# A four-layer graph network on one core: boundaries of layers 1 and 2, rows at the end, and a bias moved from TensorE to VectorE

## The reference

```
layer 0  Wh = h@W; p = softmax(leaky(s_i + d_j), masked); attn@Wh, and a dense branch with gates
layer 1  agg = (adj @ h) / deg;            out = agg @ W.T + b
layer 2  h = h@W; p = softmax(leaky(e_src_i + e_dst_j), masked); out = elu(p @ h)
layer 3  S = (X@Wq)@(X@Wk).T, masked with adj + I; out = softmax(S) @ (X@Wv)
```

## Time and profile before

| what | value |
|---|---|
| three runs, median (lowest to highest) | 2343.1 us (2340.27 to 2345.26) |
| the profiled execution, its own time | 2346.69 us |
| its span | 2345.0 us |
| PE busy | 2225.0 us (95%) |
| DVE busy | 1798.9 us (77%) |
| ACT busy | 1372.6 us (59%) |
| opening and layer 0 | 0 to 921.9 us |
| layer 1 (its block) | 921.9 to 1207.5 us |
| layer 2, to its last `ag` row | 1207.5 to about 1641 us |
| layer 3, rest | to 2345.0 us |

### The profile page before, as it was taken

One profiled execution on the slowest core, in us unless ns is written; L12 is line 12 of the kernel. 1 busy time (PEld: TensorE's weight loads), 2 busy tenths in 40 slices (PEclk: granted clock), 3 DMA queues, 4 the chain that ended last, 5 costly groups with the idle time before them and its releaser, 6 DMA issues. The chain is left out here.

```text
span 2345.0 us, 45615 instructions
## 1 busy us (share of the span) xinstructions
PE 2225.0 (95%) x17180; PEld 1701.0 (73%) x17180; DVE 1798.9 (77%) x2845; ACT 1372.6 (59%) x2100; POOL 114.6 (5%) x124
## 2 busy tenths in 40 slices
PE   5799999999999998999978999999999999999998
PEld 4677767778677776888867888887466666666667
DVE  6877788797877855212249999997898898898896
ACT  6555565665656565666655555554365565665556
POOL 2000010010100001000000000000000000000000
PEclk9899999999999999999989999999999999999999
DMA  7542340414321112222211222222111011111000
GB/s 178 113 64 37 64 82 32 82 46 82 56 62 47 39 57 84 83 89 89 89 38 58 68 67 72 79 73 85 54 37 50 26 52 52 35 46 50 25 30 28
DMA packets 62934, 146.72 MB, mean 63 GB/s; under 512 B 10023, under 2 KB 14778, under 8 KB 61757
## 3 DMA queue, kind: packets, MB, share of 16 engines
q1 hardware_dynamic: 56461, 110.57, 15.2%
q0 software_dynamic: 5760, 33.56, 8.7%
q10 hardware_dynamic: 560, 0.52, 0.1%
HBM read 170.30 MB, written 41.43 MB: 90 GB/s over the span
## 5 line engine op out<-in xcount | busy, mean ns | idle before, releaser
L193 PE MATMUL bank<-s_row,kT_hi 128*128 128x512 f16 x1024 | 308.0, 383 | 5.3 <-ACT arena L2038 3.1
L2152 PE MATMUL bank<-VB,arena 128*128 128x257 f16 x1024 | 281.8, 275 | 26.1 <-DVE arena L2078 20.1
L1560 PE MATMUL bank<-VA,ph 128*128 128x257 f16 x1024 | 281.2, 275 | 8.7 <-DVE VA L1169 8.7
L2859 PE MATMUL bank<-VA,w_dense 128*128 128x257 f16 x1024 | 280.7, 274 | 3.0 <-ACT w_dense L2683 2.4
L1562 PE MATMUL bank<-VA,pl 128*128 128x257 f16 x1024 | 280.8, 274 | 0.0
L1561 PE MATMUL bank<-VA,ph 128*128 128x257 f16 x1024 | 280.8, 274 | 0.0
L2155 PE MATMUL bank<-VB,arena 128*128 128x257 f16 x1024 | 280.7, 274 | 0.0
L2153 PE MATMUL bank<-VB,arena 128*128 128x257 f16 x1024 | 280.6, 274 | 0.0
L2861 PE MATMUL bank<-VA,arena 128*128 128x257 f16 x1024 | 280.2, 274 | 0.0
L2860 PE MATMUL bank<-VA,w_dense 128*128 128x257 f16 x1024 | 280.2, 274 | 0.0
L2017 ACT CAST arena<-arena 128x512 f16<-128x512 f32 x256 | 155.8, 617 | 153.4 <-DVE arena L2069 144.1
(11 more groups left out here) (344 smaller groups left out, 4935.9 us busy)
## 6 DMA issues: line engine op xcount, KB each, us to landing
mask<-mask_d SPq DMA_DIRECT2D x128, 256.0 KB, 2.7
arena<-mask_d SPq DMA_DIRECT2D x128, 256.0 KB, 2.7
mask_d<-in_adj POOLq DMA_DIRECT2D x8, 2048.0 KB, 23.4
xg<-in_x SPq DMA_DIRECT2D x8, 512.0 KB, 12.8
x<-xg SPq DMA_DIRECT2D x8, 512.0 KB, 3.9
xg<-x SPq DMA_DIRECT2D x8, 512.0 KB, 4.3
x<-xo POOLq DMA_DIRECT2D x8, 512.0 KB, 3.0
w_dense<-x SPq DMA_DIRECT2D x8, 512.0 KB, 4.3
```

The costliest lines, as they stand in the source:

```text
L193: last = nc.tensor.matmul(out_ap, st, mv, start=(i == 0), stop=(i == len(todo) - 1))
L1560: nc.tensor.matmul(acc, ph[:, u % HR, c], v_row(V, 0, t), start=(t == 0), stop=False)
L2152: nc.tensor.matmul(acc, p_hi, v_at(V, 0, t), start=first, stop=False)
L2859: nc.tensor.matmul(acc, ph[:, u % ring, j, c], v_row(V, 0, t), start=(t == 0), stop=False)
```

## The change

Five edits. (1) The p tiles of layer 0 and the mask rings of layers 1, 2 and 3 become one tile, `quad_ring`; so the last quad of masks of layer 1's first group is loaded in layer 0's block, as soon as the p tiles are free, and layer 1 doesn't load it again; PE takes this quad tile by tile and not by banks. (2) Wq and Wk are loaded behind layer 1's loop and not before it. (3) In layer 2, `late` is 1: the reciprocals, the `ag` rows and the ELU's Relu come one quad later in the order of DVE and ACT; `arena` is smaller by the masks. (4) The last two pairs of layer 3 are summed bank by bank, and each bank is inverted, scaled and added in one go by DVE and stored by SP (128 KB). (5) Layer 1's bias is loaded once, spread over the partitions, and added to `xg` by DVE; the ones product goes.

```diff
+        quad_ring = sb(top, "quad_ring", [P, R * GW], F32)
...
+        quad_masks = quad_ring[:, :].bitcast(U8).rearrange("p (a n) -> p a n", n=R * GW)
...
-                p32 = sb(mem, "p32", [P, PR, GW], F32)
+                p32 = quad_ring[:, :].rearrange("p (t n) -> p t n", t=PR)
...
                                 load_later()
+                                sp.wait_ge(low.sem, low.upto(G * T - 1))
+                                slot = NEXT % R
+                                sp.dma_start(quad_masks[:, slot, :], mask_d[0:P, NEXT * QW:(NEXT + 1) * QW]
+                                             ).then_inc(s_mask[slot], 16)
...
-                mask = quad_masks(arena[0]) if weighted else sb(mem, "mask", [P, MS, R * GW], U8)
+                mask = quad_masks
                 ring = 4 if weighted else 2
-                late = 0 if weighted else 0
+                late = 1 if weighted else 0
...
                         eng, stage = (dve_q, "p32") if weighted else (act_q, "hi")
+                        if not weighted and isinstance(g, int):
+                            return
...
-                    groups(sp, quad, work["sync"], None, work.get("sync_between"))
+                    if "sync_before" in work:
+                        work["sync_before"](sp)
+                    groups(sp, quad, work["sync"], None, None, work.get("sync_beside"))
...
-                        if q == 0:
+                        if q == late:
                             work["sums_free"](act, g)
                             for r in range(R):
                                 act.wait_ge(dve_s.sem, dve_s.at(g, "rden", r))
...
                             dve.wait_ge(dve_q.sem, dve_q.before(n, "lo", r))
-                            if r == 2 and q == 1 and not isinstance(g, int):
-                                inverse(g - 1, R - 1, R)
                             nc.vector.scalar_tensor_tensor(
...
                         if not isinstance(g, int):
                             middle(g - 1, q)
                         for r in range(R):
+                            if r == 1 and q == late and not isinstance(g, int):
+                                inverse(g - 1, R - 1, R)
                             dve.wait_ge(act_q.sem, act_q.at(n, "hi", r))
                             nc.vector.tensor_tensor(pl[:, slot(q, r), :], p32[:, r, :], ph[:, slot(q, r), :],
...
                     def middle(g, q):
+                        if q == late and not isinstance(g, int) and weighted:
+                            inverse(g, 0, R - 1)
...
-                        if q == 0:
-                            inverse(g, 0, R if isinstance(g, int) or not weighted else R - 1)
+                        if q == 0 and (isinstance(g, int) or not weighted):
+                            inverse(g, 0, R)
...
                     def quad(g, q):
-                        if q == Q - 1 or (q == 0 and not weighted):
+                        own = isinstance(g, int) and not weighted
+                        if (q == Q - 1 and not own) or (q == 0 and not weighted):
...
                                 last = tile_row(q, r, i)
+                                if q * R + r == T - 1 and i < R - 1:
+                                    last.then_inc(pe_r.sem, pe_r.one("row", i))
...
-            def sync_between():
+            def sync_before(sp):
+                sp.dma_start(b1[:, :], a["L1_gnn_b"].partition_broadcast(P)).then_inc(s_b1, 16)
+
+            def sync_beside(q):
+                if q >= 0:
+                    return
                 for i, src in enumerate(("L3_gnn_Wq", "L3_gnn_Wk")):
                     nc.sync.dma_start(qk32[:, i, :, :], a[src].rearrange("(k p) n -> p k n", p=P)).then_inc(s_later, 16)
 
...
                 if q == 3:
+                    dve.wait_ge(s_b1, 16)
                     dve.wait_ge(s_xin, g * 16 + (first_in + 16))
+                    nc.vector.tensor_tensor(four_rows(xg), four_rows(xg),
+                                            b1[:, :].unsqueeze(1).broadcast_to([P, R, D]), ALU.add
+                                            ).then_inc(dve_s.sem, dve_s.one("xb"))
                     dve.wait_ge(s_xout, g * 16 + stores)
                     dve.sem_inc(s_pass[0], 1)
+                    dve.wait_ge(dve_s.sem, dve_s.at(g, "xb"))
...
-                                 [(cols(aT, k, r), w("W1", k)) for k in range(K)], "W1"
+                                 [(cols(aT, k, r), w("W1", k)) for k in range(K)]
...
-                if q == 0:
+                if q == 1:
                     act.wait_ge(act_s.sem, act_s.at(g, "ag", R - 1))
                     nc.scalar.activation(e[:, :], ag[:, :], ACT.Relu, scale=-1.0).then_inc(act_s.sem, act_s.one("below"))
-                if q == 1:
...
-                sp.wait_ge(s_out, 16 * G)
+                for r in range(R):
+                    sp.wait_ge(end_rows.sem, end_rows.upto(r))
+                    sp.dma_start(out[(G - 1) * P:G * P, r * D:(r + 1) * D], row(res, r)).then_inc(s_end, 16)
+                sp.wait_ge(s_out, 16 * (G - 1))
+                sp.wait_ge(s_end, 16 * R)
...
+                def end_row(r):
+                    dve.wait_ge(end_summed.sem, end_summed.upto(r))
+                    if r == 0:
+                        dve.wait_ge(ranked.sem, ranked.upto((G - 1) * R - 1))
+                        dve.wait_ge(s_xg, 16 * G)
+                        dve.wait_ge(s_out, 16 * (G - 1))
+                    nc.vector.reciprocal(rden[:, r:r + 1], bank[4 + r][:, D:D + 1]).then_inc(end_inverted.sem, 1)
+                    dve.wait_ge(end_inverted.sem, end_inverted.upto(r))
+                    nc.vector.scalar_tensor_tensor(out=row(res, r), in0=bank[4 + r][:, 0:D], scalar=rden[:, r:r + 1],
+                                                   in1=row(xg, r), op0=ALU.mult, op1=ALU.add).then_inc(end_rows.sem, 1)
...
-                    rows(G - 1)
+                    for r in range(R):
+                        end_row(r)
...
+                def end_values(pair_list):
+                    pe.wait_ge(low.sem, low.upto(pair_list[-1]))
+                    for i in range(R):
+                        acc = bank[4 + i][:, 0:D + 1]
+                        c = slice(i * P, (i + 1) * P)
+                        for u in pair_list:
+                            for j in range(2):
+                                t = 2 * (u % pairs) + j
+                                nc.tensor.matmul(acc, ph[:, u % ring, j, c], v_row(V, 0, t), start=False, stop=False)
+                                nc.tensor.matmul(acc, ph[:, u % ring, j, c], v_row(V, 1, t), start=False, stop=False)
+                                last = nc.tensor.matmul(acc, pl[:, u % ring, j, c], v_row(V, 0, t), start=False,
+                                                        stop=(t == T - 1))
+                        last.then_inc(end_summed.sem, 1)
...
-                    for n in range(head, total + depth):
+                    for n in range(head, total + depth - 2):
                         step(n)
+                    end_values([total - 2, total - 1])
```

More of the change, by code:

```diff
@@ L2640, in sp_program @@
                 load_x(G - 1)
-                sp.wait_ge(s_out, 16 * G)
+                for r in range(R):
[3 more added lines that the diff above has]
+                sp.wait_ge(s_end, 16 * R)
             def pool_program(pool):
-                for g in range(G):
+                for g in range(G - 1):
                     pool.wait_ge(finished.sem, finished.upto(g))
@@ L2699, in step @@
                         row_of_tops(g - 1)
-                    if p == 2 and g >= 2:
+                    if p == 2 and 2 <= g <= G:
                         rows_out(g - 2)
```

22 lines of the change are left out of this document (12 added, 10 removed).

## The result

The changed kernel takes 2322.12 us (median of 4 runs, 2319.32 to 2324.34) where the kernel before, timed beside it, took 2343.94 (4 runs, 2340.27 to 2345.26): ratio 0.9909, 95% interval [0.9892, 0.9926]. A second series gave 2322.24 (5 runs), ratio 0.9913 [0.9899, 0.9926]. 2323 was forecast. The total is right, in part by luck: of its terms one was worth nothing in the whole, and another was too small.

A forecast was written before the change was run, and what follows sets the result against it. PE's work and waits were taken to bound nearly everything, with layer 2's pass set by the boundary's order. Terms 4.4 + 2.8 + 9.3 + 3.1 = 19.6 from the median 2343.1 gave 2323.5, stated as 2323; 8-in-10 range 2316 to 2333.

The forecast's parts named there:

- Edit 3, forecast 9.3: Layer 2's boundaries: the later order saves 1.5 us at each of six and 0.3 at the first, 9.3 in all.
- Edit 1, forecast 4.4: Layer 1's start: early mask and PE's order bring the transposes from 936.63 to 932.2, 4.4 us; bounds 2.4 and 5.2.
- Edit 2, forecast nothing: Loads of Wq and Wk move to SP's free time behind layer 1's loop: worth nothing.
- Edit 5, forecast 2.8: Layer 1: PE sheds 32 products, 3.1 us in the loop; the chain ends about 0.3 later; net 2.8.
- Edit 4, forecast 3.1: Kernel's end: only one bank's work remains and its store lands in 2.6 us; 3.1 saved, bounds 1.8 and 5.
- the fixed 1.26: Kernel's end: the span ends 1.26 us after the last store lands, kept as a fixed tail.
- Rival A: Layer 2: PE drops to the lower clock at every boundary; 15 us slower, 2358; chance 3%.
- B: Layer 2: PE's wait for `ag` comes back in full, no gain there, the rest 10.3; 2333 us; chance 13%.
- C: Layer 1's start gains little, the next mask or DVE's split being late; 15 to 17 in all, 2327; chance 12%.
- D: Both DVE waits in layer 2 go, no clock dips, the last store lands fast; 24 gained, 2319; chance 12%.

The follow-up runs named there:

- x10: The changed kernel run and profiled again, with nothing changed: 2322.24 us, ratio 0.9913.
- x9: The changed kernel with one more VectorE operation ahead of layer 1's loop (b1 multiplied by 1.0): 2322.80 us, ratio 0.9910.
- x4: The changed kernel with the last mask quad loaded inside layer 1's block again and PE's first quad there by banks: 2324.69 us, ratio 0.9918.
- x5: The changed kernel with the early mask kept, but PE's order in layer 1's first quad by banks again: 2321.71 us, ratio 0.9913.
- x12: The changed kernel with one 512 KB store by SP behind the last row instead of four of 128 KB: 2323.02 us, ratio 0.9915.
- x6: The changed kernel with the loads of Wq and Wk issued ahead of layer 1's loop again: 2322.31 us, ratio 0.9911.
- x2: The changed kernel with layer 1's bias made by PE as a product with the ones again: 2321.79 us, ratio 0.9903.
- x11: The changed kernel with layer 1's bias by PE, a second time, timed beside the unchanged repeat: 2320.68 us, ratio 0.9906.
- x1: The changed kernel with layer 2's boundary order undone (reciprocals, `ag` rows and Relu back in their old places): 2330.31 us, ratio 0.9944.

## Why the prediction was right, and where it was not

- **Edit 3, forecast 9.3.** Right in mechanism, and in size within 1 us. Its stage shortened by 10.14 in the first profile of after and by 8.6 against x10's; undoing it costs 8.1 in the timed runs. The six passes between boundaries went from 307.99 to 298.47, 9.52 us, but not in equal parts: the five regular ones gave 1.35 each, where 1.5 was forecast, and the first 2.78, about half of that because a clock dip of before (at 1286.9) is missing there; in x10 that pass gave 1.6. The period came at 49.70 for 49.6, L2504 followed the low tile's products, Exp was late next by 0.70, and PE waits 1.04 at quad 0, all as said. The missing 0.1 is the 0.12 of the step in x9, which no row of before could show.
- **Edit 1, forecast 4.4.** Right: 4.3 to 4.5 in layer 1's block (x4). The working did not split it: 3.8 is the mask, 0.5 to 0.7 the order (x5). Its steps, an aggregate at 928.4 and 3.5 us of products, add up to 931.9 and not to the 932.2 that the sum went by; measured from the block's start the transposes came where 932.2 puts them, at 10.3 (x10: 10.4; x12: 11.4).
- **Edit 2, forecast nothing.** Wrong by 1 to 2 us in its stage (x6): with the first mask early, the next transfer on SP's queue became the one that is late.
- **Edit 5, forecast 2.8.** This is the term that failed, and its bounds of 1.7 to 3.1 did not hold what the whole shows, 0 or a little below (-0.4 in x2, -1.5 in x11). The pass got its 0.44 and the block 2.6 to 3.2, so the working was right where it looked. The step that failed is that it took the stages behind as unmoved. They gave back 1.0 in layer 2 and 0.3 in layer 3, and in these profiles dips of the clock the rest. Of the 1.0, the 0.6 of the five regular passes goes with the step that x9 restored; the 0.4 of the first pass and the 0.3 of layer 3 are open. That the dips come from the edit and not by chance is not shown: there are only two profiles with the bias on PE.
- **Edit 4, forecast 3.1.** Too small by 1.7: 4.83. Landing was taken as 2.6 and is 1.8; the fixed 1.26 was kept and is 0.45 with SP's queue. I took the rest behind the landing for a property of the program's end, where it was one of POOL's queue, and the earlier trace rows could not tell the two.
- **The rest.** The profiled span fell by 24.9, the timed medians by 21.8. 1.38 of the difference lies ahead of layer 1 and 2.55 in layer 3, where no edit was to save time. In layer 3 before has dips at 1635 and 1693 us, after one at 1618; in layer 0 before has two (at 17 and 126 us) that after lacks. The undone edits add up to 15.4 to 16.9 of the timed 21.8 (8.1 + 6.3 + 2.5, less up to 1.5 for the bias); the other 5 to 6 are not attributed.
- **Rival A** (PE at half clock at each boundary): no. The clock read 1.00 in every regular period, with PE's wait of 1.04 and, in x1, with one of 2.54. **B** is excluded by the period of 49.70 and by x1, **C** by the block's 4.4. Part of **D** came true at the end.

That the forecast of 2323.5 came within 1.4 us of the measured 2322.12 is luck in part: edit 4's surplus of 1.7 and what no edit explains made up for edit 5.

## What to carry to other kernels

Price an edit in its own stage, and then check the stages that it doesn't touch: here the 3 us that layer 1 saved vanished in the total. A later loop took 0.12 us more in each pass, with the same instructions, and clock dips fell otherwise. A total that agrees with the forecast doesn't confirm its terms. When a transfer is taken off the path, write down which one on the same queue is next, and what is issued ahead of it. Profile the same kernel twice before you read a difference of 1 us in a stage as an edit's: x12 and the changed kernel differ by 1.0 us at layer 1's start, where their code is the same. At a kernel's end look at three things apart, what is computed behind the last product, the size of the last store, and the queue that issues it.

## What was not expected of the hardware

- A VectorE step took 0.22 instead of 0.12 us, in each pass, and one operation and one semaphore more ahead of the loop took that back (x9); no wait is shown for it.
- A store of 128 KB lands in 1.8 us by SP and 2.1 by POOL, one of 512 KB in 2.6 and 2.9; the span ends 0.45 us behind the landing of a last store by SP and 1.25 to 1.4 behind that of one by POOL.
- The granted clock's dips of some us come in one profile of a program and not in the next (x10), at the first group of layer 2 or of layer 3; two profiles of one kernel differ by 1.2 to 1.3 us in such a stage.
